# Graph network kernel, last stage: SyncE issues all bucket loads ahead of the output stores, and the grouped 62-lane stores go as 48 and 14 lanes

## Chip, cores and metric

The kernel runs as one program on one core of a Trainium2 chip. The metric is the device time of the program in microseconds (us); the time given is the median of three runs. The profile is one execution, recorded by the hardware profiler, and its span is measured from the first recorded instruction to the last.

## What is computed

Two graph layers over 6250 nodes with 48 channels each and 206250 directed edges (200000 drawn ones in both directions and one self loop a node), each followed by a residual sum and a layer norm:

```python
x = _layernorm(x + _L0_gnn_ref(x, edge_index, 6250), axis=-1)
x = _layernorm(x + _L1_gnn_ref(x, ...), axis=-1)

# second layer, cut
gate = silu(edge_attr @ W1.T + b1) @ W2.T + b2 + adapt_logit
msg  = gate * h[dst] * (cw * mj)[:, None]
agg  = segment_sum(msg, src, N) / clip(segment_sum(mj, src, N), 1e-08)
x    = h + agg                       # then a layer norm with gamma and beta
```

The output is 6250 rows of 48 float32 numbers, 192 bytes a row.

## The kernel before

The kernel sorts nothing on the host; it works in stages. Early stages build node tables and place every edge in a slot of DRAM by its source node (`slots`). The long middle stage goes over 101 tiles of 2048 edges, computes the messages and scatters them into `slots`. The change touches only the last stage, the block that begins with `RS = 5`.

**Buckets.** The nodes are cut into 51 buckets (`NB`). A bucket stands for 124 nodes: 62 (`H`) in lanes 0 to 61 and 62 in lanes 64 to 125 of the 128 partitions; the lanes between are empty. For each bucket, edge messages lie in `slots`, and one load brings them into one of five buffers (`rows`, `RS = 5`), 128 partitions by 10360 bytes.

**A turn.** For bucket `b`, ScalarE copies the key column out of the buffer (`mine`, L1582) once the load has landed. VectorE compares it with a counting tile and makes `onehot` (L1646), 4480 elements in each of 128 partitions. TensorE sums the bucket with 35 matmuls (L1689) and then frees the row buffer through the semaphore `used`. Three turns later ScalarE copies the sums to SBUF (`three`, L1561), VectorE reduces them (`most`, L1603) and GpSimd adds what the middle stage had summed already (`agg`, L1669).

**Waves.** Beside the turns, in groups of eight buckets (`WAVES`: six groups of eight and one of three), the averages, the residual and two layer norms are done. `beside(turn, (stage, lag), ...)` runs a stage for the wave that ends at bucket `e` in turn `e + lag`. VectorE does `complete_average` at lag 3, `spread(0)` at 5, `residual` at 10 and `spread(1)` at 12. GpSimd raises to the power -0.5 (`mean`, L1664), and ScalarE scales the rows of `y` (L1573) at lag 15 and signals `ready`. The wave's rows of `y` then are final.

**SyncE.** The queue of SyncE issues both the loads and the stores, in program order. Ahead of load `b` it waits until the buffer is free. In turn `e + 20` it stores the wave:

```python
for b in range(TURNS + RS):
    if b < NB:
        if b >= RS:
            e.wait_ge(used, b - RS + 1)
        e.dma_start(rows[:, b % RS]..., slots[...]).then_inc(rows_in[b % RS], 16)
    ...
    beside(b, (store, 15 + RS))
```

`store` waits for `ready`, and then for each half of the lanes issues one store of 62 lanes by one bucket (L1526, 11.6 KB) and one of 62 lanes by seven buckets (L1532, 81.4 KB; a descriptor moves one 192-byte row). A wave of eight buckets so goes in four stores with 992 rows, the last wave of three in five stores with 326 rows. The first bucket, and the last one in the upper half, are cut, since 6250 nodes do not fill them. At the end SyncE waits until all stores have landed, and the program ends.

The stage has a second branch (`when(e, 0)`) for inputs that the buckets do not hold; with these inputs it is not taken.

Of the kernel before, what the change touches and what calls it, by code (L numbers as in the profile page):

```python
# [13 lines left out]
P = 128  # L14
NODES = 6250
# [11 lines left out]
H = 62  # L27
SHIFT = 28
NP2 = (NT + 2) // 2
NB = NP2  # L30
# [7 lines left out]
R = CLASSES * S  # L38
# [4 lines left out]
CAP = 256  # L43
CLEAR = 192
CLEAR_EDGE = 128
EARLY = 96
# [79 lines left out]
def build(nc, x, src, dst, edge_attr, edge_weight, node_type, node_vec, W1T, b1, W2T, b2,  # L126
# [9 lines left out]
    slots = nc.dram_tensor("slots", (PERM * R, RC), BF16).ap()  # L136
# [4 lines left out]
    with ctx:  # L141
        def sb(name, shape, dt=F32, to=ctx):
            return to.enter_context(nc.sbuf_tensor(name, shape, dt))
# [4 lines left out]
        def sem(name, to=ctx):  # L148
            return to.enter_context(nc.semaphore(name))
# [43 lines left out]
        with ExitStack() as ph:  # L193
# [27 lines left out]
            half = sb("half", [P, NP2], F32, ph)  # L221
# [333 lines left out]
        @contextmanager  # L555
        def when(e, value):

            flag = e.value_load(near[0:1, 0:1], min_val=0, max_val=1)
            with e.If(flag == value):
                yield  # L560

        x1 = base
        with ExitStack() as ph:
# [18 lines left out]
            y = sb("y", [P, C], F32, ph)  # L582
# [687 lines left out]
        with ExitStack() as ph:  # L1270
# [20 lines left out]
            y = sb("y_f", [P, NP2, C], F32, ph)  # L1291
            square = sb("square_f", [P, NP2, C], F32, ph)
            rows = sb("rows_far", [P, NP2, TW], F32, ph)
# [178 lines left out]
        with ExitStack() as ph:  # L1472
            RS = 5
            OS = 3
            WAVE = 8
            WAVES = [(a, min(a + WAVE, NB - 3)) for a in range(0, NB - 3, WAVE)] + [(NB - 3, NB)]
            rows = sb("rows", [P, RS, COLS, RC], BF16, ph)
# [7 lines left out]
            y = sb("y1", [P, NP2, C], F32, ph)  # L1485
# [4 lines left out]
            rows_in = [sem(f"rows_in{s}", ph) for s in range(RS)]  # L1490
            keyed, ohs, used, summed, reduced, added = (sem(n, ph) for n in (
                "keyed_r", "ohs", "used_r", "summed_r", "reduced_r", "added_r"))
            v, shifted, ready, early_in_stored, normal = (sem(n, ph) for n in (
                "v1", "shifted1", "ready1", "stored1", "normal1"))
# [3 lines left out]
            def beside(turn, *stages):  # L1498


                for k, (a, b) in enumerate(WAVES):
                    for stage, lag in stages:
                        if turn == b + lag:
                            stage(k, a, b)
            TURNS = NB + 16

            with nc.Block() as block:
                @block.sync
                def _(e):
                    stores = [0]  # L1510

                    def whole(half, k):

                        first = 2 * H * k + H * half - SHIFT
                        return first >= 0 and first + H <= NODES

                    def store(j, a, b):
                        e.wait_ge(ready, j + 1)
                        for half in range(2):
                            lanes = P // 2 * half  # L1520
                            inside = [k for k in range(a, b) if whole(half, k)]
                            for k in range(a, b):
                                first = 2 * H * k + H * half - SHIFT
                                low, high = max(0, -first), min(H, NODES - first)
                                if k not in inside[:-1] and low < high:
                                    e.dma_start(out[first + low:first + high, :], y[lanes + low:lanes + high, k, :]  # L1526
                                                ).then_inc(early_in_stored, 16)
                                    stores[0] += 1
                            if len(inside) > 1:
                                first = 2 * H * inside[0] + H * half - SHIFT  # L1530
                                n = len(inside) - 1
                                e.dma_start(out[first:first + 2 * H * n, :].rearrange("(k m) c -> m k c", m=2 * H)[0:H],  # L1532
                                            y[lanes:lanes + H, inside[0]:inside[-1], :]).then_inc(early_in_stored, 16)
                                stores[0] += 1
                    with when(e, 1):
                        for b in range(TURNS + RS):
                            if b < NB:
                                if b >= RS:
                                    e.wait_ge(used, b - RS + 1)
                                e.dma_start(rows[:, b % RS].rearrange("p a c -> p (a c)"),  # L1540
                                            slots[R * (CAP * b + EARLY):R * CAP * (b + 1), :].rearrange(
                                                "(p a) c -> p (a c)", p=P)).then_inc(rows_in[b % RS], 16)
                            if b == 0:
                                e.dma_start(early[:, :, :].rearrange("p b c -> p (b c)"), early_sums
                                            ).then_inc(early_in_stored, 16)
                                stores[0] += 1
                            beside(b, (store, 15 + RS))
                        e.wait_ge(early_in_stored, 16 * stores[0])
                    stores[0] = 0
                    with when(e, 0):  # L1550
                        for j, (a, b) in enumerate(PARTS):
                            store(j, a, b)
                        e.wait_ge(early_in_stored, 16 * stores[0])
# [190 lines left out]
```

## Time and profile before

| | |
|---|---|
| median of 3 runs | 3067.45 us (3059.66, 3067.45, 3067.46) |
| span of the profiled execution | 3050.1 us |
| the profiled execution's own time | not listed apart; the median lies 17.35 us above the span |
| busy: TensorE, VectorE, GpSimd, ScalarE | 2251.7, 2404.4, 2117.9, 1399.4 us |
| last stage, from the first load's issue | 2819.2 us to the end |
| out of it: the first store's issue | 2912.1 us |
| the last one-hot's start | 3013.3 us |
| the last load's issue | 3001.6 us |
| the last store's issue | 3045.8 us |

A time in a row of the timeline is measured from the start of the span. A group's busy time counts what its instructions ran; the idle time in square brackets is what the engine waited ahead of the instruction, with the one that released it. `SPq` is the queue of SyncE: the time of a DMA instruction there is that of issuing it, not of the transfer.

### The profile page before, as it was taken

To read this page: it belongs to the slowest core of one execution; us is meant where nothing else is said; L and a number is where in the kernel's file an instruction comes from. 1 tells how busy PE (TensorE), PEld (TensorE's weight loads), DVE (VectorE), ACT (ScalarE), POOL (GpSimd) and SP (SyncE) were. 2 spreads that over 40 slices of the span, in tenths; PEclk is the share of its full clock that TensorE was granted. 3 is DMA by queue.
4 is the path that set the end of the run, shared out by engine and by line. 5 is a ranking of instruction groups with operands and counts; after the bars stand their busy time and mean duration, and the time that the engine had idled before them with its cause. 6 is when DMAs were issued, how large, how long until landed. Compare 5 with 4: busy or idle time off the path is not lost. (4 is left out here: it accounts for less than half of the span.)

```text
span 3050.1 us, 73627 instructions
## 1 busy us (share of the span) xinstructions
PE 2251.7 (74%) x25909; PEld 1913.8 (63%) x25909; DVE 2404.4 (79%) x5424; ACT 1399.4 (46%) x2929; POOL 2117.9 (69%) x1852
## 2 busy tenths in 40 slices
PE   6970477678787787777787878787878788876674
PEld 5860366566666675666676767676666666665664
DVE  9994577778787787877788788888888888875886
ACT  7982244444444454444444444444444444444122
POOL 7506777877777777777777777777777777750241
PEclk9665688888888898888888889888888988888887
DMA  8405233344434444333454444554545444452984
GB/s 314 152 7 158 61 111 112 104 119 121 117 112 119 122 125 114 113 112 114 123 155 145 144 145 145 146 147 142 158 132 163 150 155 145 143 146 81 419 327 174
DMA packets 174620, 441.51 MB, mean 145 GB/s; under 512 B 92296, under 2 KB 92296, under 8 KB 154440
## 3 DMA queue, kind: packets, MB, share of 16 engines
q1 hardware_dynamic: 103388, 236.05, 23.4%
q0 software_dynamic: 67888, 194.98, 21.9%
q10 hardware_dynamic: 3004, 5.90, 0.6%
q8 instruction: 218, 3.57, 0.5%
q14 instruction: 122, 1.00, 0.1%
HBM read 292.51 MB, written 144.27 MB: 143 GB/s over the span
## 5 line engine op out<-in xcount | busy, mean ns | idle before, releaser
L722 POOL DMA_INDIRECT slot<-table,gidx x1616 | 1827.3, 1131 | 617.3 <-issue 606.8
L821 PEld LDWEIGHTS route<-parts,oh_r 128*128 128x128 bf16 x11312 | 758.0, 99 | 88.9 <-issue 64.1
L821 PE MATMUL route<-parts,oh_r 128*128 128x148 bf16 x11312 | 806.4, 231 | 3.4 <-DVE parts L1224 3.0
L1089 DVE TENSOR_SCALAR oh_r<-iota_r,spot 128x896 bf16<-128x896 f16 x1616 | 613.5, 450 | 75.4 <-PE route L821 75.3
L894 ACT ACTIVATE routed<-route 128x444 bf16<-128x444 f32 (+1 forms) x1010 | 508.8, 514 | 250.2 <-PE route L821 234.8
L856 PE MATMUL pwin<-slot,oh_d 128*128 128x144 bf16 x1616 | 175.6, 284 | 424.0 <-DMA slot<-table,gidx 392.1
L856 PEld LDWEIGHTS pwin<-slot,oh_d 128*128 128x128 bf16 x1616 | 153.8, 156 | 448.6 <-issue 291.6
L777 PEld LDWEIGHTS pwin<-win,oh_t 128*128 128x128 bf16 x4848 | 258.8, 115 | 180.8 <-issue 96.1
L747 PE MATMUL phid<-attr,w 80*96 80x512 f32 x404 | 285.8, 798 | 48.6 <-issue 47.7
L777 PE MATMUL pwin<-win,oh_t 128*128 128x80 bf16 (+1 forms) x4848 | 272.6, 225 | 54.4 <-ACT ssum L904 49.4
L1195 DVE TENSOR_TENSOR prod<-slot,got 128x256 f32<-128x256 f32 x202 | 84.7, 419 | 243.1 <-ACT parts L955 243.0
L759 PE MATMUL gate<-w,hid 97*128 97x96 f32 x1616 | 249.1, 303 | 1.6 <-ACT hid L882 1.6
L949 ACT ACTIVATE got<-pwin 128x640 f32<-128x640 f32 x202 | 142.2, 704 | 216.8 <-PE pwin L777 214.1
L759 PEld LDWEIGHTS gate<-w,hid 97*128 97x128 f32 x1616 | 224.4, 215 | 3.5 <-ACT hid L882 2.8
L730 POOL DMA_INDIRECT slots<-routed,sidx x101 | 123.0, 1218 | 110.2 <-ACT routed L894 73.6
L1689 PE MATMUL acc<-rows,onehot 128*128 128x147 bf16 x1785 | 139.0, 241 | 79.8 <-issue 43.2
L882 ACT ACTIVATE hid<-phid,b1c 96x512 f32<-96x512 f32 x202 | 137.8, 682 | 128.5 <-PE phid L747 125.5
L962 ACT ACTIVATE parts<-val 128x384 bf16<-128x384 f32 x202 | 104.5, 517 | 198.3 <-DVE val L1208 198.3
L1689 PEld LDWEIGHTS acc<-rows,onehot 128*128 128x128 bf16 x1785 | 133.2, 144 | 85.7 <-issue 85.6
L323 ACT ACTIVATE by_col<-oh_hi 128x832 bf16<-128x832 bf16 x101 | 179.1, 1793 | 15.9 <-DVE oh_lo L463 11.5
L1176 DVE TENSOR_TENSOR eoh<-number,emine 128x2048 bf16<-128x2048 bf16 x102 | 102.8, 1057 | 92.9 <-ACT emine L981 92.6
L1646 DVE TENSOR_TENSOR onehot<-count,mine 128x4480 bf16<-128x4480 bf16 x51 | 130.4, 2556 | 19.8 <-ACT mine L1582 19.8
(228 smaller groups left out, 3211.3 us busy)
## 6 DMA issues: line engine op xcount, KB each, us to landing
rows<-slots SPq DMA_DIRECT2D x51, 1295.0 KB, 10.1
oh_t<-dst_row SPq DMA_DIRECT2D x101, 512.0 KB
erows<-slots SPq DMA_DIRECT2D x51, 777.0 KB
attr<-in_edge_attr SPq DMA_DIRECT2D x101, 320.0 KB
slots<-zeros SPq DMA_DIRECT2D x53, 518.0 KB
slot<-table,gidx POOLq DMA_INDIRECT x1616
table<-tab SPq DMA_DIRECT2D x3, 676.0 KB, 6.0
weight_t<-weights SPq DMA_DIRECT2D x101, 8.0 KB
```

The costliest lines, as they stand in the source:

```text
L323: e.activation(by_col[:, s % OR], oh_hi[:, s % OR].rearrange("p b g -> p g b"), ACT.Copy).then_inc(laid, 1)
L722: e.indirect_dma_start(out=slot[:, s, g, :], out_offset=None, in_=table0, in_offset=bass.IndirectOffsetOnAxis(ap=gidx[:, s, g:g + 1], axis ...
L747: e.matmul(phid[:, :], w1[:, :], attr[:, s % 2, 512 * m:512 * (m + 1)], start=True, stop=True).then_inc(hidden, 1)
L759: mm = e.matmul(gate[:, 2 * C * k:2 * C * (k + 1)], hid[:, P * c:P * (c + 1)], w2[:, :], start=True, stop=True)
L777: mm = e.matmul(pwin[:, g // 4, first:first + n], oh_t[:, s % 2, m * HC + g, :], win[:, s, AT[k]:AT[k] + n], start=(k == 0), stop=(k == 2) ...
L821: mm = e.matmul(route[:, (NPH * m + phase) % 2, RC * (j - a):RC * (j - a + 1)], oh_r[:, c, slot_of, :], parts[:, s % 2, c, :], start=(c == ...
L856: mm = e.matmul(sums, oh_d[:, s % 2, :, g], rows[:, g, :], start=(g == 0), stop=(g == G - 1))
L882: e.activation(hid[0:2 * C, 512 * m:512 * (m + 1)], phid[:, :], ACT.Silu, bias=b1c[:, 0:1]).then_inc(hid_sb, 1)
L894: e.activation(routed[:, s % 2, RC * (HS * m + a):RC * (HS * m + b)], route[:, (NPH * m + phase) % 2, 0:RC * (b - a)], ACT.Copy).then_inc( ...
L949: e.activation(got[:, m].rearrange("p (b k) c -> p b k c", b=2), by_bank[:, :, :, 0:WX], ACT.Copy)
L1089: oh = e.tensor_scalar(oh_r[:, c], iota_r[:, :, :], spot[:, s % 2, c:c + 1], None, ALU.is_equal)
L1689: mm = e.matmul(acc[:, b % 2, 0:3 * MW], onehot[:, b % OS, :, c], rows[:, b % RS, c, 0:3 * MW], start=(c == 0), stop=(c == COLS - 1))
```

## The change

The store's helper is written anew. All loads are issued in one loop, in their old order and with their old waits on `used`; only then come the stores of all waves, each with its old wait on `ready`. Within a wave and a half, all whole buckets go in one group (before, the group's last bucket went by itself), and the group's 62 lanes go as two stores of 48 and of 14 lanes. What is computed, the buffers and all waits of the other engines are as before.

```diff
--- before.py
+++ after.py
@@ -1514,37 +1514,40 @@
                         first = 2 * H * k + H * half - SHIFT
                         return first >= 0 and first + H <= NODES
 
+                    def put(to, of):
+                        e.dma_start(to, of).then_inc(early_in_stored, 16)
+                        stores[0] += 1
+
                     def store(j, a, b):
                         e.wait_ge(ready, j + 1)
                         for half in range(2):
                             lanes = P // 2 * half
                             inside = [k for k in range(a, b) if whole(half, k)]
+                            if inside and 2 * H * (inside[-1] + 1) + H * half - SHIFT > NODES:
+                                inside = inside[:-1]
                             for k in range(a, b):
                                 first = 2 * H * k + H * half - SHIFT
                                 low, high = max(0, -first), min(H, NODES - first)
-                                if k not in inside[:-1] and low < high:
-                                    e.dma_start(out[first + low:first + high, :], y[lanes + low:lanes + high, k, :]
-                                                ).then_inc(early_in_stored, 16)
-                                    stores[0] += 1
-                            if len(inside) > 1:
-                                first = 2 * H * inside[0] + H * half - SHIFT
-                                n = len(inside) - 1
-                                e.dma_start(out[first:first + 2 * H * n, :].rearrange("(k m) c -> m k c", m=2 * H)[0:H],
-                                            y[lanes:lanes + H, inside[0]:inside[-1], :]).then_inc(early_in_stored, 16)
-                                stores[0] += 1
+                                if k not in inside and low < high:
+                                    put(out[first + low:first + high, :], y[lanes + low:lanes + high, k, :])
+                            if inside:
+                                first, n = 2 * H * inside[0] + H * half - SHIFT, len(inside)
+                                rows_of = out[first:first + 2 * H * n, :].rearrange("(k m) c -> m k c", m=2 * H)
+                                for m, to in ((0, H // 16 * 16), (H // 16 * 16, H)):
+                                    put(rows_of[m:to], y[lanes + m:lanes + to, inside[0]:inside[-1] + 1, :])
                     with when(e, 1):
-                        for b in range(TURNS + RS):
-                            if b < NB:
-                                if b >= RS:
-                                    e.wait_ge(used, b - RS + 1)
-                                e.dma_start(rows[:, b % RS].rearrange("p a c -> p (a c)"),
-                                            slots[R * (CAP * b + EARLY):R * CAP * (b + 1), :].rearrange(
-                                                "(p a) c -> p (a c)", p=P)).then_inc(rows_in[b % RS], 16)
+                        for b in range(NB):
+                            if b >= RS:
+                                e.wait_ge(used, b - RS + 1)
+                            e.dma_start(rows[:, b % RS].rearrange("p a c -> p (a c)"),
+                                        slots[R * (CAP * b + EARLY):R * CAP * (b + 1), :].rearrange(
+                                            "(p a) c -> p (a c)", p=P)).then_inc(rows_in[b % RS], 16)
                             if b == 0:
                                 e.dma_start(early[:, :, :].rearrange("p b c -> p (b c)"), early_sums
                                             ).then_inc(early_in_stored, 16)
                                 stores[0] += 1
-                            beside(b, (store, 15 + RS))
+                        for k, (a, b) in enumerate(WAVES):
+                            store(k, a, b)
                         e.wait_ge(early_in_stored, 16 * stores[0])
                     stores[0] = 0
                     with when(e, 0):
```

The queue of SyncE at the start of the last stage, before (`rows<-slots` are the loads, `early<-early_sums` is one load of partial sums, `out_nodes<-y` are the stores, with lanes x buckets x channels):

```order
L1540 DMA rows<-slots 128x5180
L1544 DMA early<-early_sums 128x2499
L1540 DMA rows<-slots 128x5180 x28
L1526 DMA out_nodes<-y 34x48
L1526 DMA out_nodes<-y 62x48
L1532 DMA out_nodes<-y 62x6x48
L1526 DMA out_nodes<-y 62x48
L1532 DMA out_nodes<-y 62x7x48
L1540 DMA rows<-slots 128x5180 x8
```

The same place in the changed kernel:

```order
L1542 DMA rows<-slots 128x5180
L1546 DMA early<-early_sums 128x2499
L1542 DMA rows<-slots 128x5180 x50
L1518 DMA out_nodes<-y 34x48
L1518 DMA out_nodes<-y 48x7x48
L1518 DMA out_nodes<-y 14x7x48
L1518 DMA out_nodes<-y 48x8x48
L1518 DMA out_nodes<-y 14x8x48
```

Before, 29 loads stand ahead of the first wave's stores, and eight more ahead of each of the next two waves'; now all 51 stand ahead of any store.

The end of the same queue before, the last two waves:

```order
L1526 DMA out_nodes<-y 62x48
L1532 DMA out_nodes<-y 62x7x48
L1526 DMA out_nodes<-y 62x48
L1532 DMA out_nodes<-y 62x7x48
L1526 DMA out_nodes<-y 62x48
L1532 DMA out_nodes<-y 62x2x48
L1526 DMA out_nodes<-y 62x48
L1526 DMA out_nodes<-y 16x48
L1532 DMA out_nodes<-y 62x48
```

And now:

```order
L1518 DMA out_nodes<-y 48x8x48
L1518 DMA out_nodes<-y 14x8x48
L1518 DMA out_nodes<-y 48x8x48
L1518 DMA out_nodes<-y 14x8x48
L1518 DMA out_nodes<-y 62x48
L1518 DMA out_nodes<-y 48x2x48
L1518 DMA out_nodes<-y 14x2x48
L1518 DMA out_nodes<-y 16x48
L1518 DMA out_nodes<-y 48x2x48
L1518 DMA out_nodes<-y 14x2x48
```

The last wave but one keeps four stores, with other lanes; the last wave has six in place of five, and one of 62 lanes is left in it.

## Rows read from the trace of the kernel before

**Rows 1.** The page: busy time of each engine, share of the span, instructions.

```profile
PE 2251.7 (74%) x25909; PEld 1913.8 (63%) x25909; DVE 2404.4 (79%) x5424; ACT 1399.4 (46%) x2929; POOL 2117.9 (69%) x1852
```

**Rows 2.** The chain that ended last, pieces around the second wave's stores: start, duration, what.

```profile
2943.35 10.32 SPq L1526
...
2954.26 9.13 DMA rows<-slots
```

**Rows 3.** Stretches: window, busy PE, PEld, DVE, ACT, POOL, clock, DMA share, GB/s.

```profile
127.00:132.50 5.50, 5.48 (x61) 4.79 (x60) 4.99 (x6) 5.20 (x3) 0.00 (x0) 0.50 0.95 152
2831.00:2866.00 35.00, 27.55 (x372) 26.05 (x369) 29.57 (x19) 4.85 (x21) 2.27 (x8) 0.95 1.01 423
2866.00:2912.00 46.00, 34.56 (x457) 33.39 (x458) 45.35 (x54) 13.55 (x55) 28.15 (x16) 0.93 0.97 396
2912.00:3016.00 104.00, 72.57 (x911) 69.48 (x911) 90.45 (x101) 25.71 (x105) 26.90 (x32) 0.90 0.80 312
2985.00:2991.00 6.00, 3.33 (x32) 3.21 (x31) 5.76 (x11) 0.97 (x3) 0.29 (x1) 0.74 0.20 30
...
3038.00:3047.00 9.00, 0.00 (x0) 0.00 (x0) 0.00 (x0) 0.00 (x0) 0.00 (x0) 0.50 0.18 24
```

**Rows 4.** Waits within 2912 to 3016 us: us in total, times, longest.

```profile
ACT mine L1582 <- DMA rows<-slots: 54.8, 24, 5.5
...
DVE onehot L1646 <- ACT mine L1582: 12.3, 17, 3.0
```

**Rows 5.** Waits within 2866 to 2912 us.

```profile
DVE onehot L1646 <- ACT mine L1582: 0.4, 1, 0.4
```

**Rows 6.** Groups within 2912 to 3016 us: busy us, mean ns | idle before.

```profile
L1646 DVE TENSOR_TENSOR onehot<-count,mine 128x4480 bf16<-128x4480 bf16 x26 | 66.5, 2556 | 12.3 <-ACT mine L1582 12.3
```

**Rows 7.** Timeline of VectorE, a turn without and one with a wait: start, duration, instruction.

```profile
2871.96 0.32 DVE L1603 TENSOR_REDUCE most<-three 128x49 f32<-128x147 f32 x1
2872.19 2.55 DVE L1646 TENSOR_TENSOR onehot<-count,mine 128x4480 bf16<-128x4480 bf16 x1
...
2946.00 0.32 DVE L1603 TENSOR_REDUCE most<-three 128x49 f32<-128x147 f32 x1
...
2946.56 2.56 DVE L1646 TENSOR_TENSOR onehot<-count,mine 128x4480 bf16<-128x4480 bf16 x1 [0.24 <-ACT mine L1582]
```

**Rows 8.** Timeline of the queue of SyncE, 2912 to 3002 us.

```profile
2913.18 6.75 SPq L1526 DMA_DIRECT2D out_nodes<-y  x1
...
2943.35 10.32 SPq L1526 DMA_DIRECT2D out_nodes<-y  x1
...
2977.28 9.27 SPq L1526 DMA_DIRECT2D out_nodes<-y  x1
...
3001.64 0.33 SPq L1540 DMA_DIRECT2D rows<-slots  x1
```

**Rows 9.** Timeline from 3013 us on: VectorE's last one-hot, ScalarE's last scaling, the queue of SyncE.

```profile
3013.29 2.56 DVE L1646 TENSOR_TENSOR onehot<-count,mine 128x4480 bf16<-128x4480 bf16 x1 [0.29 <-ACT mine L1582]
...
3034.32 2.58 ACT L1573 ACTIVATE y<-y,mean 128x48 f32<-128x48 f32 x11
...
3036.26 0.24 SPq L1526 DMA_DIRECT2D out_nodes<-y  x1
3036.54 0.32 SPq L1532 DMA_DIRECT2D out_nodes<-y  x1
3036.90 2.68 SPq L1526 DMA_DIRECT2D out_nodes<-y  x1
...
3045.79 0.27 SPq L1532 DMA_DIRECT2D out_nodes<-y  x1
```

**Rows 10.** DMA issues: tensors, queue, operation, count, KB each, us to landing.

```profile
rows<-slots SPq DMA_DIRECT2D x51, 1295.0 KB, 10.1
...
queries<-tab SPq DMA_DIRECT2D x1, 816.0 KB, 7.1
```

**Rows 11.** Timeline of the queue of SyncE, the fourth of four table stores.

```profile
230.30 3.01 SPq L290 DMA_DIRECT2D table<-tab  x1
```

## Prediction

> **What bounds the kernel now.** I began with the page: over the whole span VectorE is busy for 79% [rows 1], but that is a mean over stages, and the change touches the last 231 us alone. So I read only this stage: the chain that ended last, then stretches, then who waits for whom, then the queue of SyncE row by row.
>
> The chain [rows 2] runs, at 2943 us, over the queue of SyncE: issuing one 62-lane store takes 10.32 us, the load behind it lands 9.13 us after its own issue, and VectorE's next one-hot comes behind that landing. The stretches [rows 3] show three regimes. From 2831 to 2866 us the loads pace the stage: DMA share 1.01, 423 GB/s, and VectorE has gaps. From 2866 to 2912 us VectorE paces it, busy for 45.35 of 46 us; its one wait for a key column is 0.4 us [rows 5]. From 2912 us, where the first store is issued, to 3016 us VectorE is busy for only 90.45 of 104 us, and the DMA share falls to 0.80 although nothing has been taken from the loads. VectorE now waits 17 times for `mine`, 12.3 us in all, and `mine` waits for loads [rows 4]. The queue shows why: one store in each wave is issued in 6.75, 10.32 and 9.27 us [rows 8], and no load can pass it. While the stores then run, the DMA share is 0.20 and the rate 30 GB/s, in the window from 2985 us [rows 3]: most of the DMA engines stand idle while SyncE cannot feed them.
>
> The end has a bound of its own. All arithmetic is over at 3036.90 us (34.32 + 2.58) [rows 9], but the span ends at 3050.1: from 3036.26 to 3046.06 us SyncE issues nine stores, with one of them alone taking 2.68 us, and then they land.
>
> **The change, part by part.**
>
> *Loads ahead of all stores.* Up to 2912 us the two programs issue the same things in the same order, so nothing moves there. From then on a load waits for its buffer only. What VectorE loses after 2912 us is the price: 12.3 us of waits [rows 4], and a bit that the bracket doesn't hold. A turn without a wait has the one-hot start 0.23 us after the reduction (71.96 to 72.19), one with a wait of 0.24 us has it 0.56 us after (46.00 to 46.56) [rows 7]; so 0.33 us are lost where 0.24 are shown, 0.09 more a wait, times 17 = 1.5 us. Sum 13.8 us. Would the loads still be late without the stores? A load moves 1295 KB [rows 10], or 1.326 MB, at 423 GB/s [rows 3] in 3.13 us, eight in 25.1 us. VectorE made 26 one-hots from 2912 to 3016 us [rows 6], so without the waits a turn, its share of the waves' work in it, takes (104 - 13.8) / 26 = 3.47 us, eight take 27.8 us. Loads and five buffers keep ahead of that, by some 2.7 us a wave. So I take all 13.8 us; the lower bound is 6 us, if the loads stay late enough to leave half of the waits, the upper 14.5 us, if the one wait of 0.4 us [rows 5] has no like after 2912 us. The last one-hot then starts at 3013.29 - 13.8 = 2999.5 us, and the arithmetic of the last wave ends at 3036.90 - 13.8 = 3023.1 us, since the 23.6 us of work between them hang on no DMA.
>
> *Held-back stores.* Three waves' stores that went out at 2912, 2943 and 2977 us now wait for the last load, which goes out about four turns before the last one-hot, near 2990 us; its data has left the queue at the latest four loads later, 3002 us. Nobody reads `out` and nobody reuses `y`, so the delay costs nothing unless the stores drain slowly. Today they do: in the end stretch 24 GB/s from 3038 us [rows 3], at 192 bytes a row 125 rows a us, at a DMA share of 0.18. Other stores do not: the one of `queries`, 128 lanes by 51 rows of 128 bytes, ran at 152 GB/s, 1190 rows a us, with a share of 0.95 from 127 us [rows 3], and landed in 7.1 us [rows 10]. The new stores have 48 and 14 lanes, and no row of this trace has either; the bounds are 125 and 1190 rows a us. A share of 0.18 is about 3 of 16 engines, so a 62-lane store is not spread, and the diff changes just the shape; I take some 900 rows a us, three quarters of the 128-lane row, which is the only other shape of short rows with a rate here, and keep both ends for the rivals. The held-back rows of the first four waves, 3940, then take some 4.4 us from 3002 us on, and are gone by 3007 us, well before the last arithmetic ends at 3023.1 us.
>
> The Trainium skill (DMA: Bandwidth & Descriptors, section Why a DMA increments its semaphore by 16 and not by 1) gives this as a rule: the number of engines is the largest up to 16 that divides the slowest dimension of both sides, so 2 for 62 lanes, 16 for 48 and 14 for 14. By it each engine of today's stores moves about 62 rows a us, and a pair of 48 and 14 lanes by eight rows would take about 0.5 us. The share of 0.18 agrees for 62 lanes; no row here shows 48.
>
> *The end.* Two parts of it go. From 3036.90 us, when the arithmetic is over, to the end there are 13.2 us. Of the four stores of the last wave but one, three are still to be issued then, and six of the last wave. An issue that nothing holds takes 0.24 to 0.33 us [rows 8, 9]; with 0.04 us between them and the larger patterns I take 0.38. Nine of them take 3.4 us. Behind the last issue I keep what stands there now, 3050.1 - 3046.06 = 4.0 us: today it includes rows still to be drained, so it is a bound from above. The end so takes 7.4 us in place of 13.2, a gain of 5.8 us. The bounds: none, if issuing stays as long as it is; 7.3 us, if the landing shrinks to 2.5 us.
>
> The skill has a rule against this part (same page, section Rules for kernel authors): coalesce small transfers, since under 64 KB one pays mostly overhead. The 14-lane store is 21.5 KB. If such an overhead held the queue itself for 0.98 us a store, the ten last stores would take today's 9.8 us and the end would gain nothing, which is the first rival. Two issues 0.28 us apart (36.26 and 36.54) [rows 9] do not agree with it.
>
> *Sum.* 13.8 + 5.8 = 19.6 us off the profiled execution: its span goes from 3050.1 to 3030.5 us. The median of the runs lies 17.35 us above the span, and I add this unchanged: 3067.45 - 19.6 = 3047.9 us.
>
> **The rivals.**
>
> *Only the loop gains.* SyncE's issuing of ten stores at the end takes as long as now, because generating 384 descriptors over 16 engines holds it as generating 434 over few does. For it: a table store of 128 lanes by 12 buckets took 3.01 us to issue behind three others [rows 11], so a spread store can stall too. Against: it stood behind three of 13 buckets, 4992 rows, and the last two waves here are 1318 rows. Price: 3067.45 - 13.8 = 3053.7 us.
>
> *Only the end gains, or each part half.* The loads remain late since their own pace decides: they need 3.13 us where a bare turn needs 2.70. Against: 2866 to 2912 us, where VectorE was never kept waiting for more than 0.4 us [rows 5]. Price: 5.8 + 6, or less, 3055.6 to 3061.6 us.
>
> *The held-back stores become the end: slower.* All 6250 rows now begin to flow near 3002 us, where before 3000 of them had gone by 2992 us. With r rows a us and 2 us for landing, the span is 3004 + 6250/r. At today's 125, if the new shapes are spread no better, it is 3054 us, 4 us over before: no change. Below 113 rows a us it is over 0.3% slower, and if the 48-lane stores ran on a single engine, some 62 rows a us, it is 3105 us, and the time 3122 us. Against it stands the `queries` row; for it, that nobody has stored 48 lanes in this trace.
>
> *The change doesn't do what it says* can be left out: the order of the queue shows 51 loads ahead of any store.
>
> **How the numbers follow.** A measurement of this kernel tells 0.3%, 9.2 us, from no change, so faster means below 3058.2 us. Chances: both gains 0.78, only the loop 0.09, only the end or halves 0.05 (most of it under 3058), slow stores at 125 rows a us or a gain under 9.2 us 0.05, slow stores below that 0.03. So faster 0.89, same 0.07, slower 0.04. The predicted time is the first case's, 3047.9 us. Its own range is 3045.7 (14.5 + 7.3 us off) to 3053.7 by the bounds, and one run of the kernel before lay 7.8 us under the other two, so a median may come out that much lower: 3040. Upward the range takes in the rival with the loop's gain alone and most of the halves: 3057.
>
> **What would show it.** In the profile after: no gap of VectorE ahead of a one-hot from 2912 us on but for tenths; the last one-hot near 2999.5 us; the DMA share without its holes; all loads issued by about 2990 us; the last wave's stores issued between 3023 and 3027 us with no issue over 1 us; stores at a DMA share well over 0.2; the span near 3030.5 us. It is wrong if VectorE waits for `mine` again in each wave, if the queue of SyncE still shows issues of 2 us and more after 3023 us, or if the last arithmetic ends later than 3027 us.

## The result, and the profile after

The changed kernel takes 3040.36 us (median of 6 runs, 3027.21 to 3046.97) against 3067.05 us (6 runs, 3059.66 to 3079.56): the ratio is 0.9907, with a 95% interval from 0.9881 to 0.9932, so 28.5 us less of 3067 us, within 21 to 36.5 us. The forecast was 19.6 us less. It moved as forecast, but by the ratio 1 us further than the range allowed (27.5 us at most). The two medians themselves lie 26.7 us apart.

The page of the profiled execution, whose span is 3025.4 us: busy time as in [rows 1].

```profile
PE 2250.1 (74%) x25909; PEld 1913.9 (63%) x25909; DVE 2404.3 (79%) x5424; ACT 1395.5 (46%) x2929; POOL 2121.9 (70%) x1852
```

The busy times are those of before within 4 us: what changed is waiting. Stretches of the last stage, with the columns of [rows 3]:

```profile
2831.00:2866.00 35.00, 26.94 (x383) 25.60 (x381) 30.57 (x27) 5.25 (x23) 2.54 (x9) 1.00 1.01 424
2866.00:2912.00 46.00, 36.05 (x474) 34.76 (x475) 45.55 (x47) 13.64 (x55) 31.35 (x17) 0.93 0.99 396
2912.00:2996.00 84.00, 64.37 (x826) 61.84 (x825) 82.59 (x97) 25.04 (x102) 48.58 (x30) 0.90 0.93 366
...
3020.00:3022.00 2.00, 0.00 (x0) 0.00 (x0) 0.00 (x0) 0.00 (x0) 0.00 (x0) 0.50 0.53 97
```

The first two are as before. In the third VectorE is busy for 82.59 of 84 us, where it was busy for 90.45 of 104 us [rows 3]. The last shows the new stores as they drain at the end: 97 GB/s at a DMA share of 0.53, against 24 GB/s at 0.18. The waits from 2912 to 2999 us, to be held against [rows 4]:

```profile
ACT mine L1585 <- DMA rows<-slots: 7.9, 6, 1.8
...
DVE onehot L1649 <- ACT mine L1585: 0.2, 1, 0.2
```

Of 17 waits with 12.3 us one is left, of 0.2 us. The queue of SyncE, against [rows 8, 9]; rows with a count are merged, so their time is from the first issue's start to the last one's end:

```profile
2986.97 0.33 SPq L1542 DMA_DIRECT2D rows<-slots  x1
...
3018.91 0.82 SPq L1518 DMA_DIRECT2D out_nodes<-y  x2
...
3021.37 1.75 SPq L1518 DMA_DIRECT2D out_nodes<-y  x4
```

The last load goes out at 2986.97 us, in place of 3001.64. The last ten stores are issued from 3018.91 to 3023.12 us, 0.42 us each, and the span ends 2.3 us later. And the last one-hot, with the chain that follows it:

```profile
2995.97 2.54 DVE L1649 TENSOR_TENSOR onehot<-count,mine 128x4480 bf16<-128x4480 bf16 x1
...
3016.98 2.59 ACT L1576 ACTIVATE y<-y,mean 128x48 f32<-128x48 f32 x11
```

The stage began 3.5 us earlier in this profile (first load issued at 2815.69 in place of 2819.21 us), so times are best taken from there. Measured so, the last one-hot starts 180.3 us after the first load's issue and did so 194.1 us after it: 13.8 us less. From the last one-hot to the end of the span it is 29.4 us in place of 36.8: 7.4 us less. The last stage as a whole gives 21.2 us. Two questions are left: which part of the diff does it, and why the timed runs give 28.5 us.

### The profile page after: what moved, and what is told of

It is laid out like the page before. It is cut to its first block and busy times, and to the rows that moved or that the text cites. A ratio compares the mean times of both kernels' runs of the same rounds, so it can differ in the third digit from the quotient of the medians.

```text
span 3025.4 us, 73628 instructions
## 1 busy us (share of the span) xinstructions
PE 2250.1 (74%) x25909; PEld 1913.9 (63%) x25909; DVE 2404.3 (79%) x5424; ACT 1395.5 (46%) x2929; POOL 2121.9 (70%) x1852
## 5 line engine op out<-in xcount | busy, mean ns | idle before, releaser
L856 PE MATMUL pwin<-slot,oh_d 128*128 128x144 bf16 x1616 | 167.6, 276 | 404.2 <-DMA slot<-table,gidx 372.1
L949 ACT ACTIVATE got<-pwin 128x640 f32<-128x640 f32 x202 | 142.0, 703 | 230.3 <-PE pwin L777 227.0
L730 POOL DMA_INDIRECT slots<-routed,sidx x101 | 116.5, 1153 | 115.1 <-ACT routed L894 76.9
L356 PEld LDWEIGHTS deg<-by_col,oh_lo 128*128 128x128 bf16 x1616 | 108.9, 165 | 53.8 <-ACT by_col L323 53.2
```

The costliest lines, as they stand in the source:

```text
L856: mm = e.matmul(sums, oh_d[:, s % 2, :, g], rows[:, g, :], start=(g == 0), stop=(g == G - 1))
L949: e.activation(got[:, m].rearrange("p (b k) c -> p b k c", b=2), by_bank[:, :, :, 0:WX], ACT.Copy)
```

## The experiments

Theory A: what costs the time is that a store of 62 lanes drains at some 122 rows a us (the rate that the expectations use; the stretch from 3038 us in [rows 3] gives 125), which holds the queue of SyncE and with it the loads; the split mends that, the order doesn't matter. Theory B: the order does it. The table gives, for each profile, the first load's issue, the last one-hot's start and the span, all in us, and what follows for the stage, which is counted from the first load's issue to the end of the span. Each row is one profile.

| kernel | first load | last one-hot | span | one-hot after first load | stage |
|---|---|---|---|---|---|
| before | 2819.2 | 3013.3 | 3050.1 | 194.1 | 230.9 |
| changed | 2815.7 | 2996.0 | 3025.4 | 180.3 | 209.7 |
| order_only | 2833.5 | 3014.0 | 3064.0 | 180.5 | 230.5 |
| split_only | 2814.8 | 2995.0 | 3024.5 | 180.2 | 209.7 |
| lanes31 | 2846.1 | 3026.5 | 3127.9 | 180.4 | 281.8 |
| lanes58 | 2836.9 | 3018.0 | 3067.8 | 181.1 | 230.9 |
| before_again | 2806.6 | 2999.8 | 3036.9 | 193.2 | 230.3 |
| before_aa | 2815.6 | 3010.6 | 3047.4 | 195.0 | 231.8 |
| after_again | 2821.5 | 3001.5 | 3030.9 | 180.0 | 209.4 |
| tail_act | 2816.0 | 2996.1 | 3024.2 | 180.1 | 208.2 |

### One part of the change alone

*order_only* is the kernel before with the loads ahead:

```diff
-                        for b in range(TURNS + RS):
-                            if b < NB:
...
-                            beside(b, (store, 15 + RS))
+                        for b in range(NB):
...
+                        for k, (a, b) in enumerate(WAVES):
+                            store(k, a, b)
```

> All loads first, stores in their old form of 62 lanes. Theory A (the 62-lane stores drain at about 122 rows a us wherever they stand; what the split changes is that rate): the loop gains the 13.8 us, so the last one-hot starts about 180 us after the stage's first load issue, but the 6250 rows begin to flow near 176 us and take 51 us, so the stage, from its first load issue to the end of the span, takes about 229 us, as before (230.9): time within 0.3% of before. Theory B (the order carries the gain, the shape of the stores matters little): the stage takes 210 to 213 us as in the changed kernel, 18 to 21 us faster than before.

Measured: 3051.52 us against 3055.79, ratio 0.9992 (0.9971 to 1.0013), stage 230.5 us. Theory A stands, B falls. The loop gains all that it does in the changed kernel (one-hot at 180.5 us), and the end takes it back. Its stretch from 3020 to 3060 us and its queue there:

```profile
3020.00:3060.00 40.00, 0.00 (x0) 0.00 (x0) 11.04 (x34) 8.61 (x34) 7.13 (x7) 0.55 0.18 24
```

```profile
3016.92 3.41 SPq L1526 DMA_DIRECT2D out_nodes<-y  x1
...
3037.25 4.09 SPq L1526 DMA_DIRECT2D out_nodes<-y  x1
...
3053.99 3.70 SPq L1526 DMA_DIRECT2D out_nodes<-y  x1
```

For 40 us the queue moves nothing but stores, at 24 GB/s, and every second issue takes 3.4 to 4.1 us; the other engines have little left to do. All loads were issued before 3005.4 us, so from 3017 us on the hold is the stores' own drain: a pair of them is 496 rows, and nine pairs are issued from 3016.92 to 3053.99 us, one every 4.1 us, 120 rows a us.

In the kernel before, loads stand ahead of the stores in the same queue, and the long issue there is not all lost. Two stretches, one from the middle and one around the end of the 10.32 us issue (2943.35 to 2953.67 us [rows 8]):

```profile
2947.00:2949.00 2.00, 1.66 (x26) 1.51 (x24) 2.00 (x1) 0.00 (x0) 0.00 (x0) 1.00 0.98 414
2953.00:2955.00 2.00, 0.63 (x6) 0.66 (x7) 1.93 (x5) 0.02 (x1) 0.29 (x1) 0.69 0.18 23
```

In the first, the loads ahead still move, at 414 GB/s. From about 2952 to 2957 us only the stores do, at 23 GB/s: the next load is issued at 2954.26 us, behind them, and lands 9.13 us later [rows 2]. That hole is what VectorE then waits for.

*split_only* is the changed kernel with the old loop, the same lines of the diff the other way round.

> Loads and stores in their old order, stores of 48 and 14 lanes. Theory A (what held the queue of SyncE was the slow drain of the 62-lane stores): no store in the loop is issued in over 1.5 us, a wave's 992 rows drain in under 2 us, VectorE waits little more than in the changed kernel, and the stage takes 210 to 213 us: the time is that of the changed kernel within 0.1%. Theory B (a store ahead of a load delays it even when it drains fast, since it stands in the same queue): holes in the loads remain after 92 us of the stage, VectorE waits for 4 to 8 us more, the stage takes 215 to 219 us.

Measured: 3026.26 us against 3055.79, ratio 0.9904 (0.9882 to 0.9926), stage 209.7 us, as the changed kernel to 0.1 us. Theory A again. Two details of the expectation missed, at no cost: two store issues took 2.35 and 1.67 us, not under 1.5, and a wave did not drain in under 2 us, since loads move beside it (the second wave is issued at 2935.85 us, and its last rows land at 2946.2). Its stretch, and the queue at the first two waves' stores:

```profile
2912.00:2996.00 84.00, 62.84 (x830) 59.97 (x829) 82.76 (x97) 25.62 (x102) 50.99 (x31) 0.94 0.95 368
```

```profile
2907.57 4.12 SPq L1518 DMA_DIRECT2D out_nodes<-y  x5
2911.74 24.06 SPq L1543 DMA_DIRECT2D rows<-slots  x8
2935.85 3.17 SPq L1518 DMA_DIRECT2D out_nodes<-y  x4
```

SyncE is held for 4.12 and 3.17 us, and for 1.99 us by the third wave, not for 8.4 us (2912.06 to 2920.44), 11.6 and 10.5 us. The loads behind it land later than in the changed kernel (ScalarE waits for them 15 times from 2907 to 2999 us, 21.6 us in all, against 6 times and 7.9 us), but no one-hot waits any more: the prediction's 2.7 us a wave, by which the loads keep ahead, and the buffers take it up. The reordering, half of the diff, is worth nothing that shows here once the stores are spread.

### Is it the number of lanes

Both are the changed kernel with other pieces of the 62 lanes.

```diff
-                                for m, to in ((0, H // 16 * 16), (H // 16 * 16, H)):
+                                for m, to in ((0, H // 2), (H // 2, H)):      # lanes31
+                                for m, to in ((0, 58), (58, H)):              # lanes58
```

> The changed kernel, but 62 lanes go as 31 and 31. Theory A with the skill's rule on the number of engines (DMA: Bandwidth & Descriptors: the largest number up to 16 that divides the lanes): 31 lanes run on one engine, all stores on the same one, at about 61 rows a us; 6250 rows from 176 us of the stage on take 102 us, so the stage takes about 280 us, some 50 us more than before. Theory C (a store drains slowly by its number of rows or by how it is laid out in DRAM, not by its lanes): the half-size stores drain at 122 rows a us or faster, the stage takes 229 us or less.

Measured: one run of 3129.68 us, stage 281.8 us, where the expectation was 280. Theory C falls. The stretch from 3040 to 3120 us:

```profile
3040.00:3120.00 80.00, 0.00 (x0) 0.00 (x0) 5.38 (x16) 5.85 (x24) 3.34 (x3) 0.50 0.09 12
```

12 GB/s at a share of 0.09, half of the 62-lane stores' 24 at 0.18.

> The changed kernel, but the 62 lanes go as 58 and 4. As many stores, and about as unequal, as with 48 and 14. By the skill's rule on divisors (DMA: Bandwidth & Descriptors) 58 lanes get 2 engines and 4 lanes get 4: the two lowest engines carry some 3020 rows each at 61 rows a us, so from 176 us of the stage on 50 us, and the stage takes about 228 us, as before. If instead smaller stores or one more store a group are what helps, the stage takes 209 to 213 us.

Measured: one run of 3069.62 us, stage 230.9 us, 3 us over the 228 expected and 18 to 22 us over the other case. The stretch from 3020 to 3060 us:

```profile
3020.00:3060.00 40.00, 2.93 (x42) 2.67 (x40) 14.86 (x44) 9.61 (x37) 8.62 (x10) 0.59 0.19 24
```

As many stores as in the changed kernel, now of 87 and 6 KB, and the old rate: the number of stores is not it. Nor is their size: those of lanes31 have 46.5 KB, less than the 81.4 KB of the kernel before, and go at half its rate. With 31, 58, 62 and 48 lanes at 12, 24, 24 GB/s and (with 14 beside it) 97 GB/s, these runs agree with the Trainium skill (DMA: Bandwidth & Descriptors, section Why a DMA increments its semaphore by 16 and not by 1), by which 31 lanes get one engine, 58 and 62 get two, and 48 sixteen. The Trainium skill's advice on the same page to coalesce small transfers (section Rules for kernel authors) would have chosen the slower shape here; the measurement decides.

The engines can also be counted, since the traces hold every increase of the stores' completion semaphore. Behind the 16 of the one early load (128 lanes) there are 103 in the kernel before and in order_only, 456 in the changed kernel and in split_only, 78 in lanes31 and 134 in lanes58. All four numbers come out exactly if each store gives one increase for every engine that it runs on, and one more if these are fewer than 16. With 2 engines for 62, 58 and 34 lanes, 1 for 31, 4 for 4, 14 for 14 and 16 for 48 and 16 lanes, the kernel before has 29 stores of 3 and one of 16 (103). The changed one has 14 of 16, 14 of 15, 2 of 3 and one of 16 (456); lanes31 has 28 of 2, lanes58 14 of 3 and 14 of 5, and each the same last three (78, 134). So the cause is the number of engines, and not only a rate that goes with the lanes. The DMA share is no such count: it stands at 0.09 of 16, or 1.5, with one engine at work.

### Where the other 7 us come from

> The kernel before, unchanged, for a second profile. Its last stage, from first load issue to the end of the span, takes 230 to 232 us again, if that stage is steady from run to run; the part ahead of it is what spreads (2819 us in the first profile, 2816 us in that of the changed kernel), by some 10 us either way. If the stage itself spreads by several us, the 21.2 us between the two profiles' last stages are less sure.

Measured: 3038.68 us, span 3036.9, stage 230.3 us, within 0.6 us of the first profile; the part ahead of it is 12.6 us shorter. Here the time of the profiled execution itself is known: 1.8 us above its span.

> The kernel before, unchanged, timed against itself. Theory D (the part of the measured gain beyond the last stage's 21.2 us is spread of the earlier stages from run to run): the ratio departs from 1 by as much as 0.2%, on either side, and its interval is as wide as the changed kernel's was (0.5%). Theory E (the change also moved something ahead of the last stage): the ratio stays within 0.1% of 1, and the extra 7 us are real.

Measured: ratio 1.000 (0.9982 to 1.0017), stage 231.8 us. That is the ratio that Theory E named, and the interval, 0.35% wide, is narrower than D had it.

> The changed kernel, unchanged, timed again. Its last stage takes 209 to 211 us. Theory D: the ratio lies nearer 0.9931, which 21.2 us of 3060 give, than 0.9907; its profile's part ahead of the last stage falls anywhere between 2806 and 2846 us, where those of the earlier profiles fell. Theory E: the ratio is 0.9907 again within 0.05%, and the part ahead of the stage is some 7 us shorter than that of the kernel before in its profile.

Measured: 3037.98 us against 3057.99, ratio 0.9934 (0.9909 to 0.9960), or 20.2 us; stage 209.4 us, with 2821.5 us ahead of it. So the same kernel was measured at 28.5 and at 20.2 us faster, with the stage's 21.2 us between. The part ahead of the stage, in three profiles of the kernel before and four of kernels with spread stores, is 2807 to 2819 and 2815 to 2822 us: no gain shows there. In the other three profiles, order_only, lanes31 and lanes58, it is 2834 to 2846 us, with the same program ahead of the stage, so single profiles spread by 40 us there and can't tell 7. Theory D fits the changed kernel: its two intervals both take in 0.9931, and the second ratio is not E's 0.9907. Not all is settled: before_aa came out as E named, and split_only's interval ends at 0.9926, 1.4 us beyond what its stage shows. Whether some part of a few us ahead of the stage is real stays open.

### The end bound by issuing

*tail_act*: SyncE issues the lower half of the last two waves, ScalarE, behind its last scaling, the upper half with helpers of the same text.

```diff
 # SyncE
-                            store(k, a, b)
+                            store(k, a, b, (0, 1) if k < len(WAVES) - 2 else (0,))
+                        stores[0] += 5
 # ScalarE, behind its loop
+                        for k in (len(WAVES) - 2, len(WAVES) - 1):
+                            store(k, *WAVES[k], (1,))
```

> The changed kernel, but ScalarE issues the upper half's stores of the last two waves, five of the ten. Theory (the end of the changed kernel is bound by the issuing of ten stores on one queue, 0.42 us each, 4.2 us, and by 2.3 us behind the last): from the end of the last scaling to the end of the span it takes 4.4 us in place of 5.8, and the stage 208.3 us; in the ratio this is lost. Rival (the two queues share what makes the descriptors, so five and five take as long as ten): 5.8 us or more, stage 209.7.

Measured: 3034.71 us against 3057.99, ratio 0.9922 (0.9894 to 0.9951), with after_again at 0.9934 in the same comparison. The stage takes 208.2 us, as expected to 0.1 us. ScalarE at the end:

```profile
3019.12 0.55 ACT L1605 ACTIVATE y<-y,mean 128x48 f32<-128x48 f32 x2
3019.43 2.10 ACTq L1569 DMA_DIRECT2D out_nodes<-y  x4
```

From the end of the last scaling (3019.67) to that of the span (3024.2) it is 4.5 us in place of 5.8. In after_again the same stretch is 5.8 us again. So this is the fastest version of the study by its stage, by 1.2 to 1.5 us, which the timed runs can't tell.

## Why the prediction was right or wrong

**Loads ahead of stores, 13.8 us: right, size and place.** The last one-hot came 13.8 us earlier against the first load, and VectorE paced the loop to its end. But the gain was put down to the wrong part of the diff: the prediction named the order, and split_only shows that the shape alone gives the same 13.8. The order alone gives it too (order_only), but the end then takes it back.

**Held-back stores drain fast: right, though not as fast as forecast.** I took 900 rows a us between bounds of 125 and 1190, and 4.4 us for the 3940 rows of the first four waves. Their 17 stores took 10.4 us to issue (2987.35 to 2997.72 us), 380 rows a us; at the end the stores went at 97 GB/s, or 505 rows a us, with the issue of 0.42 us a store as their pace. It cost nothing: their last rows land at 2999.0 us, where the forecast had 3007. The share of 0.18 was read as about 3 of 16 engines; the semaphore counts show 2. The slow rival named here was real: order_only is just its case of 125 rows a us, forecast at a span 4 us longer, measured at a stage 0.4 us shorter; and lanes31 is its case of a single engine, forecast at 55 us more by the span (3105), measured at 51 more by the stage.

**The end, 5.8 us: too small by 1.6.** Issuing was right: nine stores at 0.38, 3.4 us, measured 3.55 from the end of the arithmetic (3019.57) to the last issue's end (3023.12), with 0.42 us a store. The term that was mis-sized is the one kept behind the last issue, 4.0 us; it measured 2.3. In the kernel before, the last rows land 2.7 us behind the last issue, in the changed kernel 1.0 us, and in both the span ends 1.3 us after that: the prediction's 4.0 held rows still to be drained, which it said and did not take off.

**The sum, 19.6 us, against 21.2 in the stage and 28.5 in the timed runs.** The first difference is the term above, and with it alone the time would lie well inside the range. The step that failed is the spread term of the range: "one run of the kernel before lay 7.8 us under the other two, so a median may come out that much lower: 3040". That took the spread of a whole comparison from three runs of one kernel, and it took it off the middle value, 3047.9, and not off the bound that the parts had given, 3045.7, which would have made 3037.9. The first ratio puts the time at 3067.45 x 0.9907 = 3038.9 us. The runs showed in its place that the same kernel comes out 28.5 us faster in one comparison and 20.2 us in the next, that six runs of the changed kernel spread over 19.8 us in the first, and that the kernel before ran from 3043.04 to 3079.56 us in all comparisons together. So the first ratio is 7.3 us of luck or of something ahead of the stage, which stays open, on top of a gain that the stage shows.

"The median of the runs lies 17.35 us above the span, and I add this unchanged" did no harm to the gain, since it stands on both sides, but it was misread. The executions recorded later lie 1.8 us above their spans. If the first one did too, it ran some 15 us faster than its median, and those 17.35 us were mostly spread, a sign that 7.8 us was too little.

**The rivals.** "Only the loop gains" fell: ten stores are issued in 4.2 us, where nine took 9.8. "Only the end gains" fell with the waits gone.

## What to carry to other kernels

Count the lanes of a store before its bytes: 62 lanes of 192-byte rows left at 24 GB/s, 58 too, 31 at 12, and the same rows in 48 and 14 lanes at 97. A long issue of a DMA on the queue of SyncE was here the drain of what stood ahead of it, and whatever stood behind it, the loads, started late; mending the drain was enough, and mending the order alone gained nothing. And where a change touches one stage of a long program, measure that stage in the profiles: it repeated within 0.3 us (changed kernel) and 1.5 us (kernel before), where whole runs of one kernel spread by 20 to 37 us. A range for such a program has to allow for that spread on both sides of the comparison.

## What was not expected of the hardware

GpSimd's small sums got slower on average when VectorE lost its gaps. Groups of the last stage, first of the kernel before, then of the changed one:

```profile
L1669 POOL TENSOR_TENSOR agg<-most,early 128x49 f32<-128x49 f32 x51 | 37.2, 729 | 136.8 <-DVE most L1603 136.8
```

```profile
L1672 POOL TENSOR_TENSOR agg<-most,early 128x49 f32<-128x49 f32 x51 | 60.6, 1189 | 96.5 <-DVE most L1606 96.5
```

The same 51 instructions on the same tiles took 729 ns on average before and 1189 ns after. The kernel before shows both kinds already; its one-hots beside them are in [rows 7], from 2872.19 and from 2946.56 us:

```profile
2872.35 2.54 POOL L1669 TENSOR_TENSOR agg<-most,early 128x49 f32<-128x49 f32 x1 [5.29 <-DVE most L1603]
...
2946.40 0.27 POOL L1669 TENSOR_TENSOR agg<-most,early 128x49 f32<-128x49 f32 x1 [2.89 <-DVE most L1603]
```

The first starts 0.16 us after a one-hot and ends at 2874.89 us, 0.15 us after that one-hot does; the second starts 0.16 us ahead of its one-hot and takes 0.27 us. It is so for all 51 sums of both kernels. Each that starts while a one-hot runs ends 0.12 to 0.15 us after it, however early it started (1.1 to 2.5 us long). The others take 0.26 to 0.30 us, or 0.52. Before, 11 of the 51 start within a one-hot, in the changed kernel 24: the sum is released by the reduction, and where VectorE waits for `mine` behind it, the sum is through before the one-hot starts. So the sum is not slower in itself; it waits for the one-hot, as far as these rows tell, and no run here varied the two instructions. It costs nothing here, since VectorE waits for the sums once, 1.1 us at the end, in both kernels, but a kernel with GpSimd's sums on the path would give back part of what it gained on VectorE.
